# Lag attention on sums and differences of mirrored rows

## The chip, the cores and the metric

The kernel runs on one core of one Trainium2 chip. The metric is the device time of one execution in microseconds; the time before is 1598.67 us, the median of three runs (1595.01 to 1599.94).

## The reference

Two blocks of a gated cross-attention model run on x (8 batches, 256 positions, 1024 features) and a context of the same shape. The change lies in the first operation only, an attention over lags: the normalised x is correlated with the context along the sequence in each feature, the eleven largest lags of the 256 are found, softmaxed, and used to add up shifted copies of the context.

```python
qf = jnp.fft.fft(q, axis=2)
kf = jnp.fft.fft(k, axis=2)
corr = jnp.fft.ifft(qf * jnp.conj(kf), axis=2).real
topk = int(C * np.log(L))                     # 11, with C = 2 and L = 256
w, idx = jax.lax.top_k(corr.transpose(0, 1, 3, 2), topk)
w = jax.nn.softmax(w, axis=-1)
for i in range(topk):
    g = jnp.minimum(idx[:, :, None, :, i] + pos, L - 1)
    out = out + w[:, :, None, :, i] * jnp.take_along_axis(v, g, axis=2)
...
x = x + jnp.tanh(g_xattn[0]) * _L0_xattn_ref(_layernorm(x, axis=-1), ctx_4096, ctx_4096)
x = x + jnp.tanh(g_ffn[0]) * _L0_ffn_ref(...)      # 16 experts, 2 per token
x = x + jnp.tanh(g_xattn[1]) * _L1_xattn_ref(...)  # attention over the context
x = x + jnp.tanh(g_ffn[1]) * _L1_ffn_ref(...)      # quantised feed-forward
```

After that come a mixture of experts, a softmax attention over the context, and a quantised feed-forward. Rows (positions) are independent of each other in all of these but for the pairing of a batch's queries with its own context.

## The kernel before

x stays in SBUF for the whole kernel (tile X, 16 tiles of 128 rows by 1024). The function lag_attention treats 16 units: a unit u is a batch b = u // 2 and a half h of the features (512 columns, C). The Fourier transforms are float32 matrix products with tables held in `tab`. Each product of a 128x128 table with 512 columns appears in the profile as two records, and all of them are issued by the helper at L52.

One unit passes through these steps. `spectra` on the tensor engine (L454) transforms the context (v_raw) and the normalised queries (q_n): the table has four kinds (even cosine, even sine, odd cosine, odd sine) and the 256 rows are two blocks, so 8 products for the context (4 for the even kinds, then 4 for the odd ones, into the same PSUM banks 2 and 3) and 4 for the queries (banks 0 and 1). The scalar engine copies the context's spectra into `vs` (L276 to L289; the even ones are four instructions and signal v_ev1). `c_products` on the vector engine (L340) multiplies the spectra, `c_sums` on GpSimd (L233) adds them, `correlate` (L473) transforms back to lags, `lags_out` (L291) copies the result to `corr`. `top_lags` on the vector engine (L347) works on four groups c of 128 features: two rounds of the eight largest, masking, and `finish`, which multiplies the exponentials (`exponent`, scalar engine, L297) by a mask, takes the reciprocal of the sum and scales (L360). `turn_weights` (L484) transposes the weights by the tensor engine, `weights_out` (L302) copies them, `weight_spectra` (L492) transforms them by 8 products into banks 4 to 7. `o_products` (L398) multiplies these with `vs` in 8 instructions, `o_sum` (L241) adds pairs on GpSimd, `positions` (L500) transforms back to rows by 8 products, and `add` (L408) adds the result to X. Each second unit the vector engine also forms the layer-norm tables of a batch (`variance`, `tables`), for the first norm of a batch to come or for the running norm of a batch that is done; one power on GpSimd lies between the two.

Each engine's order is written out by hand in its function `step`; in a step `now` is unit u, `before` is u-1, `after` is u+1, `next2` is u+2:

```python
# vector engine: top_lags(now) in two halves, o_products(before) between them,
#                c_products(after), add(before), variance and tables
# tensor engine: spectra(after), positions(before), turn_weights(now),
#                correlate(after), weight_spectra(now)
# scalar engine: lags_out(now) x2, exponent(now) 0 and 1, spectra(after, even),
#                exponent(now) 2 and 3, spectra(after, odd), normalise(next2) x2, weights_out(now)
# GpSimd:        o_sum(before) x4, c_sums(after), powers of the norms
```

An instruction waits for semaphores only; an engine never passes a waiting instruction. In particular `spectra(after, even)` on the scalar engine waits until all 8 `o_products(before)` are done, since both units use the same slot of `vs` (the units u-1 and u+1 have the same h), and `c_products(after)` waits for v_ev1. At the start the whole `tab` (3584 columns, 1.8 MB) comes in one transfer, ahead of the gate's value.

## Time and profile before

| | |
|---|---|
| median of three runs | 1598.67 us |
| the profiled execution | 1598.1 us, span 1596.4 us |
| lag attention in it | from the start to about 529 us |
| tensor engine busy in the span | 1360.1 us (85%) |
| vector engine busy | 797.0 us (50%) |
| scalar engine busy | 523.3 us (33%) |
| GpSimd busy | 428.1 us (27%) |

The busy shares are means over stages that differ. In lag attention the pattern of a unit repeats about every 30 us. A row of the timeline merges equal neighbouring instructions: the first number is the start, the second the time from the first one's start to the last one's end, "x8" how many, and in brackets is how long the engine stood idle before and what released it. "PEclk" is the tensor engine's granted clock as a share of 2.4 GHz: 1.00 is 2.4 GHz, 0.50 is 1.2 GHz. A row of windows gives the stretch and its length, then busy time (and instructions) of the tensor engine's matmuls, its weight loads, the vector engine, the scalar engine and GpSimd, then the granted clock, the DMA share and GB/s.

### The profile page before, as it was taken

To read this page: it belongs to the slowest core of one execution; us is meant where nothing else is said; L and a number is where in the kernel's file an instruction comes from. 1 tells how busy PE (TensorE), PEld (TensorE's weight loads), DVE (VectorE), ACT (ScalarE), POOL (GpSimd) and SP (SyncE) were. 2 spreads that over 40 slices of the span, in tenths; PEclk is the share of its full clock that TensorE was granted. 3 is DMA by queue.
4 is the path that set the end of the run, shared out by engine and by line. 5 is a ranking of instruction groups with operands and counts; after the bars stand their busy time and mean duration, and the time that the engine had idled before them with its cause. 6 is when DMAs were issued, how large, how long until landed. Compare 5 with 4: busy or idle time off the path is not lost. (4 is left out here: it accounts for less than half of the span.)

```text
span 1596.4 us, 19695 instructions
## 1 busy us (share of the span) xinstructions
PE 1360.1 (85%) x6035; PEld 894.1 (56%) x6041; DVE 797.0 (50%) x2181; ACT 523.3 (33%) x827; POOL 428.1 (27%) x481
## 2 busy tenths in 40 slices
PE   5999999999996799898888788259999999927886
PEld 2454454454452674346666576158888888714443
DVE  3678778778774444002122122265444442227996
ACT  2322322322320420004344344322222222148884
POOL 1223223223222002502111112361111100035885
PEclk9999999999997868999899999679999999968999
DMA  4210210400200623005667665433332321060111
GB/s 178 79 54 27 79 53 26 171 13 14 93 1 0 226 94 104 15 0 184 191 209 234 207 216 184 156 92 118 106 101 87 101 67 53 27 217 27 53 53 79
DMA packets 53378, 159.14 MB, mean 100 GB/s; under 512 B 7120, under 2 KB 15312, under 8 KB 53200
## 3 DMA queue, kind: packets, MB, share of 16 engines
q1 hardware_dynamic: 41792, 120.20, 21.4%
q0 software_dynamic: 11536, 38.30, 8.1%
q8 instruction: 28, 0.46, 0.1%
q14 instruction: 22, 0.18, 0.0%
HBM read 112.82 MB, written 45.66 MB: 99 GB/s over the span
## 5 line engine op out<-in xcount | busy, mean ns | idle before, releaser
L44 PE MATMUL xa_bank<-xa_xT_hi,M_hi 128*128 128x256 f32 x512 | 153.7, 300 | 0.0
L46 PE MATMUL xa_bank<-xa_xT_hi,M_lo 128*128 128x256 f32 x512 | 144.2, 282 | 0.0
L45 PE MATMUL xa_bank<-xa_xT_lo,M_hi 128*128 128x256 f32 x512 | 144.2, 282 | 0.0
L52 PE MATMUL la_bank<-la_v_raw,la_tab 128*128 128x512 f32 x256 | 118.5, 606 | 29.5 <-ACT la_v_spec L285 16.3
L1026 PEld LDWEIGHTS ex_bank<-ex_gu,ex_xT 128*128 128x128 f32 x624 | 119.6, 194 | 22.4 <-issue 20.9
L52 PE MATMUL la_bank<-la_osum,la_tab 128*128 128x512 f32 x256 | 117.4, 613 | 13.8 <-POOL la_osum L246 13.8
L1026 PE MATMUL ex_bank<-ex_gu,ex_xT 128*128 128x224 f32 x624 | 127.3, 358 | 0.7 <-ACT ex_xT L961 0.7
L246 POOL TENSOR_TENSOR la_osum<-la_oprod 128x512 f32<-128x512 f32 x64 | 82.7, 1313 | 153.4 <-DVE la_oprod L405 153.4
L52 PE MATMUL la_bank<-la_wT,la_tab 128*128 128x512 f32 x256 | 112.6, 592 | 1.2 <-ACT la_wT L306 1.2
L52 PEld LDWEIGHTS la_bank<-la_v_raw,la_tab 128*128 128x128 f32 x256 | 48.0, 192 | 96.1 <-issue 55.8
L1212 ACT ACTIVATE xa_A<-xa_bank,shift 128x256 f32<-128x256 f32 x64 | 30.3, 473 | 209.7 <-PE xa_bank L46 209.7
L44 PEld LDWEIGHTS xa_bank<-xa_xT_hi,M_hi 128*128 128x128 f32 x512 | 97.0, 189 | 2.8 <-issue 1.7
L45 PEld LDWEIGHTS xa_bank<-xa_xT_lo,M_hi 128*128 128x128 f32 x512 | 97.0, 190 | 2.5 <-issue 1.7
L46 PEld LDWEIGHTS xa_bank<-xa_xT_hi,M_lo 128*128 128x128 f32 x512 | 96.8, 189 | 0.0
L988 DVE COPY ex_xT<-ex_bank 128x512 f32<-128x512 f32 x40 | 27.7, 692 | 138.4 <-PE ex_bank L1008 138.4
L1038 PE MATMUL ex_bank<-ex_dn,ex_silu_then_turned 112*128 112x512 f32 x156 | 83.1, 658 | 14.3 <-ACT ex_silu_then_turned L973 14.3
L52 PEld LDWEIGHTS la_bank<-la_osum,la_tab 128*128 128x128 f32 x256 | 50.2, 197 | 78.8 <-issue 63.3
L602 PE MATMUL ex_bank<-Wk,Wq 128*128 128x512 f32 x192 | 88.7, 624 | 6.5 <-issue 4.8
L405 DVE TENSOR_TENSOR la_oprod<-la_bank,la_v_spec 128x512 f32<-128x512 f32 x128 | 80.1, 685 | 18.2 <-PE la_bank L52 7.8
L933 POOL TENSOR_TENSOR ex_current<-ex_listed,ex_nought 128x1 int32<-128x1 int32 x41 | 7.7, 188 | 271.6 <-PE ex_bank L1008 268.6
L52 PEld LDWEIGHTS la_bank<-la_wT,la_tab 128*128 128x128 f32 x256 | 48.6, 190 | 55.8 <-issue 53.6
L999 DVE COPY ex_y<-ex_bank 128x512 f32<-128x512 f32 x39 | 27.0, 692 | 102.7 <-ACT ex_y L976 102.7
(264 smaller groups left out, 2684.5 us busy)
## 6 DMA issues: line engine op xcount, KB each, us to landing
produced<-ex_y SPq DMA_DIRECT2D x39, 512.0 KB, 3.0
ex_gu<-in_gate_up SPq DMA_DIRECT2D x16, 896.0 KB, 6.2
X<-in_x SPq DMA_DIRECT2D x8, 1024.0 KB, 7.1
la_v_raw<-in_ctx SPq DMA_DIRECT2D x16, 512.0 KB, 4.3
produced<-la_zeros SPq DMA_DIRECT2D x16, 512.0 KB, 5.2
normal<-rt_xn SPq DMA_DIRECT2D x16, 512.0 KB, 3.6
xa_fT<-in_ctx_T SPq DMA_DIRECT2D x8, 1024.0 KB, 5.6
xa_f<-in_ctx SPq DMA_DIRECT2D x8, 1024.0 KB, 5.0
```

The costliest lines, as they stand in the source:

```text
L44: pe.matmul(out, a[0], b[0], start=first, stop=False)
L45: pe.matmul(out, a[0], b[1], start=False, stop=False)
L46: return pe.matmul(out, a[1], b[0], start=False, stop=last)
L52: return pe.matmul(out, a, b, start=first, stop=last)
L246: pool.tensor_tensor(osum[:, i, :], oprod[:, a, :], oprod[:, a + 1, :], ALU.add if i % 2 == 0 else ALU.subtract).then_inc(s["osums"], 1)
L405: dve.tensor_tensor(oprod[:, 2 * (i % 2) + k, :], bank[bk][:], vs[:, h, vk, :], ALU.mult).then_inc(s["oprods"], 1)
L602: last = pe.matmul(out, W[1][:, k, (n // 2) * P:(n // 2 + 1) * P], W[0][:, k, (n % 2) * 512:(n % 2 + 1) * 512], start=(k == 0), stop=(k == ...
L988: dve.tensor_copy(xT[:, 4:8, :].rearrange("p a b -> p (a b)"), bank[3][:]).then_inc(s["xT_dve"], 1)
L999: dve.tensor_copy(y[:, 512:1024], bank[5][:]).then_inc(s["y_dve"], 1)
L1026: m = pe.matmul(bank[0][:, 0:UP_COLS], xT[:, k, :], gu[:, slot, k * UP_COLS:(k + 1) * UP_COLS], start=(k == 0), stop=(k == KD - 1))
L1038: m = pe.matmul(bank[4 + i][:], hT, dn[:, slot, i * 512:(i + 1) * 512], start=True, stop=True)
L1212: act.activation(A[:, m % AHEAD, :], bank[2 + m % 2][:, 0:L], ACT.Identity, bias=shift[:, m:m + 1]).then_inc(s["a_out"], 1)
```

## The change

The second half of every batch (rows 128 to 255) of x and of the context is laid down in falling order before the launch, and the result is turned back after it. Row p of the one block then lies beside its mirror image in the other, so the cosine kinds need only the sum of the blocks and the sine kinds only the difference. GpSimd forms the sums and differences of context, queries and weights (`v_halves`, `q_halves`, `w_halves`). What the mirror does not cover (the last row of the context, lag 0 and lag 128) goes in by products with a single row, and one by a full product with `sign_t`. The back transform gives two banks, whose sum is one block and whose difference is the other: `add` has four instructions, not two. Products (each is two records) per unit: context 8 to 6 (two of them with one row), queries 4 to 2, weights 8 to 6 (one with one row), positions 8 to 4.

The scaling of the weights (L360) goes from the vector to the scalar engine (`share`), `c_products` moves into the middle of `top_lags`, `correlate` ahead of `turn_weights`, `lags_out` to the step before, `positions` starts when two of the four sums are there, and the table comes in two transfers (896 columns, then 1664).

```diff
+        v_less = sb("v_less", [P, 2, C])
+        q_less = sb("q_less", [P, C])
+        w_less = sb("w_less", [P, 4, P])
...
-            sp.dma_start(tab[:], tables).then_inc(s["tab_in"], 16)
+            sp.dma_start(tab[:, 0:LAGS_AT], tables[:, 0:LAGS_AT]).then_inc(s["tab_in"], 16)
             sp.dma_start(graw[:], column(gate, 0)).then_inc(s["gate_in"], 16)
             load_v(1, 0, 1)
+            sp.dma_start(tab[:, LAGS_AT:], tables[:, LAGS_AT:]).then_inc(s["tab_rest"], 16)
...
+            def v_halves(u, b, h):
+                pool.wait_ge(v_in[h], 16 * (b + 1))
+                pool.tensor_tensor(v_less[:, h, :], v_raw[:, h, 0, :], v_raw[:, h, 1, :], ALU.subtract).then_inc(s["v_fold"], 1)
+                pool.tensor_tensor(v_raw[:, h, 0, :], v_raw[:, h, 0, :], v_raw[:, h, 1, :], ALU.add).then_inc(s["v_fold"], 1)
+            def q_halves(u):
+                pool.wait_ge(s["q_ready"], 2 * u + 2)
+                pool.tensor_tensor(q_less[:], q_n[:, 0, :], q_n[:, 1, :], ALU.subtract).then_inc(s["q_fold"], 1)
+                pool.tensor_tensor(q_n[:, 0, :], q_n[:, 0, :], q_n[:, 1, :], ALU.add).then_inc(s["q_fold"], 1)
+            def w_halves(u, g):
+                pool.wait_ge(s["wdone"], 4 * u + 2 * g + 2)
+                two = slice(2 * g, 2 * g + 2)
+                a, b = wt[:, two, 1:P], wt[:, two, P + 1:L]
+                pool.tensor_tensor(w_less[:, two, 1:P], a, b, ALU.subtract).then_inc(s["w_fold"], 1)
+                pool.tensor_copy(w_less[:, two, 0:1], wt[:, two, P:P + 1]).then_inc(s["w_fold"], 1)
+                pool.tensor_tensor(a, a, b, ALU.add).then_inc(s["w_fold"], 1)
...
             def step(on, due):                      # GpSimd
+                if next2:
+                    v_halves(*next2)
                 if before:
                     for i in range(4):
                         o_sum(before[0], i)
                 if after:
                     c_sums(after[0])
+                if now:
+                    w_halves(now[0], 0)
+                    w_halves(now[0], 1)
+                if next2:
+                    q_halves(next2[0])
...
-                at_least(act, s["wdone2"], 4 * u)
+                at_least(act, s["wdone2"], 4 * (u - 1) + 2 * g + 2)
...
+            def share(u, c):
+                act.wait_ge(s["wrec"], 4 * u + c + 1)
+                act.activation(wt[:, c, :], wt[:, c, :], ACT.Identity, scale=wrec[:, c:c + 1]).then_inc(s["wdone"], 1)
...
             def step(on, due):                      # scalar engine
                 if now:
-                    lags_out(now[0], 0)
-                    lags_out(now[0], 1)
                     exponent(now[0], 0)
                     exponent(now[0], 1)
                 if after:
                     spectra(after[0], after[2], False)
                 if now:
-                    exponent(now[0], 2)
-                    exponent(now[0], 3)
+                    share(now[0], 0)
                 if after:
                     spectra(after[0], after[2], True)
                 if next2:
                     for j in range(2):
                         normalise(*next2, j)
                 if now:
+                    exponent(now[0], 2)
+                    share(now[0], 1)
+                    exponent(now[0], 3)
+                    share(now[0], 2)
+                if after:
+                    lags_out(after[0], 0)
+                if now:
+                    share(now[0], 3)
+                if after:
+                    lags_out(after[0], 1)
+                if now:
                     weights_out(now[0])
...
-                    return dve.tensor_scalar(w, w, wrec[:, c:c + 1], None, ALU.mult)
...
-                    count("wdone", finish(c - 1, 2))
+                    dve.memset(spare[:], 0.0)
...
+                for i, signs in enumerate(((tg, tg), (tg, less_tg))):
+                    if i:
+                        at_least(dve, s["half_added"], 2 * u + 2)
+                    for j in range(2):
+                        xs = X[:, bass.ds(2 * b + j, 1), halfsl(h)]
+                        made = dve.scalar_tensor_tensor(out=xs, in0=bank[4 + i][:].rearrange("p (a c) -> p a c", a=1), scalar=signs[j][:, 0:1],
+                                                        in1=xs, op0=ALU.mult, op1=ALU.add)
...
                 def output_spectra():
                     if before:
                         o_products(before[0], before[2])
+                    if after:
+                        c_products(after[0], after[2])
                 if now:
                     lags(now[0], output_spectra)
                 else:
                     output_spectra()
-                if after:
-                    c_products(after[0], after[2])
...
+                at_least(pe, s["v_fold"], 2 * u + 2)
                 at_least(pe, s["corr_sb"], 2 * u)
+                full_product(pe, bank[2][:], rows_t(0), more, True, False)
+                full_product(pe, bank[2][:], last_t(0), last, False, True)
+                full_product(pe, bank[3][:], rows_t(1), less).then_inc(s["spec_v1"], 1)
+                at_least(pe, s["q_fold"], 2 * u + 2)
                 at_least(pe, s["prods"], 4 * u)
+                full_product(pe, bank[0][:], rows_t(0), q_n[:, 0, :])
+                full_product(pe, bank[1][:], rows_t(1), q_less[:]).then_inc(s["spec_q"], 1)
                 at_least(pe, s["v_ev1"], u + 1)
+                full_product(pe, bank[2][:], rows_t(2), more, True, False)
+                full_product(pe, bank[2][:], last_t(1), last, False, True)
+                full_product(pe, bank[3][:], rows_t(3), less).then_inc(s["spec_v2"], 1)
...
-                at_least(pe, s["wdone"], 5 * u + 5)
+                at_least(pe, s["w_fold"], 6 * u + 6)
...
+                full_product(pe, bank[4][:], lags_t(0), more, True, False)
+                full_product(pe, bank[4][:], last_t(2), first, False, True)
+                full_product(pe, bank[5][:], lags_t(1), less, True, False)
+                full_product(pe, bank[5][:], sign_t, more, False, True)
+                full_product(pe, bank[6][:], lags_t(2), more)
+                full_product(pe, bank[7][:], lags_t(3), less).then_inc(s["wspec"], 1)
...
+                for i, (j, first) in enumerate(((0, True), (1, True), (1, False), (0, False))):
+                    at_least(pe, s["osums"], 4 * u + max(i, 1) + 1)
+                    m = full_product(pe, bank[4 + j][:], pos_t(i), osum[:, i, :], first, not first)
...
                 if before:
                     positions(before[0])
+                if after:
+                    correlate(after[0])
                 if now:
                     turn_weights(now[0])
-                if after:
-                    correlate(after[0])
-                if now:
                     weight_spectra(now[0])
```

## Rows read from the trace of the kernel before

**Rows 1.** The page: its first line.
```profile
span 1596.4 us, 19695 instructions
```
**Rows 2.** Busy time by windows: the steady part, then one stretch after an idle time.
```profile
200.00:300.00 100.00, 95.95 (x278) 49.61 (x277) 79.85 (x274) 29.35 (x54) 25.83 (x22) 1.00 0.25 92
486.80:490.80 4.00, 3.98 (x5) 1.71 (x6) 3.76 (x17) 0.51 (x1) 0.00 (x0) 0.55 0.00 0
```
**Rows 3.** Timeline of one unit, vector engine.
```profile
241.84 2.48 DVE L405 TENSOR_TENSOR la_oprod<-la_bank,la_v_spec 128x512 f32<-128x512 f32 x4
246.95 0.49 DVE L356 SCALAR_TENSOR_TENSOR la_wt<-la_rest,la_wt 128x256 f32<-128x256 f32 x1
249.14 0.36 DVE L360 TENSOR_SCALAR la_wt<-la_wt,la_wrec 128x256 f32<-128x256 f32 x1
249.41 0.09 DVE L380 MATCH_VALUE_LOAD la_rest<-la_nextv,la_rest 128x8 f32 x1
249.92 0.43 DVE L356 SCALAR_TENSOR_TENSOR la_wt<-la_rest,la_wt 128x256 f32<-128x256 f32 x1
253.76 2.48 DVE L345 TENSOR_TENSOR la_prod<-la_bank,la_v_spec 128x512 f32<-128x512 f32 x4
259.97 1.41 DVE L412 SCALAR_TENSOR_TENSOR X<-la_bank,la_tg,X 128x512 f32 x2 [3.73 <-PE la_bank L52]
261.30 0.69 DVE L564 BATCH_NORM_STATS2 first_ln_stats<-X 128x6 f32 x1
266.66 0.06 DVE L352 MEMSET la_spare<- 128x1 f32 x1 [0.37 <-issue]
271.89 2.48 DVE L405 TENSOR_TENSOR la_oprod<-la_bank,la_v_spec 128x512 f32<-128x512 f32 x4
```
**Rows 4.** The same unit, tensor engine.
```profile
241.00 3.60 PE L52 MATMUL la_bank<-la_v_raw,la_tab 128*128 128x512 f32 x8
249.23 3.70 PE L52 MATMUL la_bank<-la_v_raw,la_tab 128*128 128x512 f32 x8 [1.20 <-ACT la_v_spec L285]
252.77 7.03 PE L52 MATMUL la_bank<-la_osum,la_tab 128*128 128x512 f32 x16
259.64 1.04 PE L489 MATMUL la_bank<-la_ident,la_wt 128*128 128x128 f32 x8
```
**Rows 5.** The same unit, scalar engine.
```profile
247.07 0.60 ACT L281 ACTIVATE la_v_spec<-la_bank 128x512 f32<-128x512 f32 x1 [6.63 <-DVE la_oprod L405]
252.97 0.60 ACT L288 ACTIVATE la_v_spec<-la_bank 128x512 f32<-128x512 f32 x1 [1.54 <-PE la_bank L52]
253.94 1.51 ACT L274 ACTIVATE la_q_n<-X,first_ln_shift,first_ln_scale 128x512 f32 x2
```
**Rows 6.** The same unit, GpSimd.
```profile
243.21 2.50 POOL L246 TENSOR_TENSOR la_osum<-la_oprod 128x512 f32<-128x512 f32 x2 [7.70 <-DVE la_oprod L405]
245.88 2.69 POOL L246 TENSOR_TENSOR la_osum<-la_oprod 128x512 f32<-128x512 f32 x2 [0.17 <-DVE la_oprod L405]
```
**Rows 7.** Timeline, tensor engine, work that follows an idle time.
```profile
21.98 5.40 PE L52 MATMUL la_bank<-la_q_n,la_tab 128*128 128x512 f32 x8 [4.15 <-ACT la_q_n L274]
50.64 5.11 PE L52 MATMUL la_bank<-la_tab,la_cross 128*128 128x256 f32 x16 [2.67 <-POOL la_cross L239]
486.82 8.89 PE L52 MATMUL la_bank<-la_osum,la_tab 128*128 128x512 f32 x16 [7.08 <-POOL la_osum L246]
511.64 10.13 PE L52 MATMUL la_bank<-la_osum,la_tab 128*128 128x512 f32 x16 [6.74 <-POOL la_osum L246]
```
**Rows 8.** Timeline: the start, and the output products of units 0, 13 and 15.
```profile
14.74 0.20 ACT L265 ACTIVATE la_tg<-la_graw 128x1 f32<-128x1 f32 x1 [12.63 <-DMA la_graw<-in_g_xattn]
62.71 2.48 DVE L405 TENSOR_TENSOR la_oprod<-la_bank,la_v_spec 128x512 f32<-128x512 f32 x4 [2.91 <-issue]
450.47 2.48 DVE L405 TENSOR_TENSOR la_oprod<-la_bank,la_v_spec 128x512 f32<-128x512 f32 x4 [2.91 <-issue]
504.93 2.48 DVE L405 TENSOR_TENSOR la_oprod<-la_bank,la_v_spec 128x512 f32<-128x512 f32 x4 [7.77 <-PE la_bank L52]
```

More of the change, by code:

```diff
@@ L66, in fourier_tables, with kinds, mirrored @@
 def fourier_tables():
-    t = np.arange(L)[:, None].astype(np.float64)
+    w = np.pi / L
+    p = np.arange(P)[:, None].astype(np.float64)
     k = np.arange(P)[None, :].astype(np.float64)
-    even, odd = 2 * np.pi * t * k / L, np.pi * t * (2 * k + 1) / L
-    alternate = (-1.0) ** np.arange(L)
-    seq = np.stack([np.cos(even), np.sin(even), np.cos(odd), np.sin(odd)], 1)
-    inverse = seq.copy() * 2.0
-    seq[:, 1, 0] = alternate
-    inverse[:, 0, 0] = 1.0
-    inverse[:, 1, 0] = alternate
-    ext = seq.copy()
-    ext[L - 1, 0, 0] += L
-    ext[L - 1, 2:] -= seq[:, 2:].sum(0)
-    lag = inverse[:, :2] / L
-    pos = inverse / (2 * L)
-    pos[:, 1, 0] *= -1.0
-    seq, ext = (x.reshape(2, P, 4, P).transpose(1, 0, 2, 3).reshape(P, -1) for x in (seq, ext))
-    lag, pos = (x.transpose(2, 1, 0).reshape(P, -1) for x in (lag, pos))
-    return np.concatenate([seq, ext, lag, pos], 1).astype(np.float32)
-TABLE_COLS = 2 * 4 * P * 2 + 2 * L + 4 * L
+    sign = (-1.0) ** np.arange(P)
+    def kinds(at):
+        return np.stack([np.cos(2 * k * w * at), np.sin(2 * k * w * at), np.cos((2 * k + 1) * w * at), np.sin((2 * k + 1) * w * at)], 1)
+    middle = p - (L - 1) / 2
+    rows = kinds(middle)
+    rows[:, 1, 0] = np.sin(np.pi * middle[:, 0])
+    last = np.zeros((3, P, P))
+    last[0, 0, 0] = L
+    last[1, 0] = -2 * rows[:, 2].sum(0)
+    last[2, 0] = sign
+    lags = kinds(p)
+    lags[:, 1, 0] = 0
+    lags[0, 1, 0] = 1
+    lags[0, 3] = -sign
+    found = np.concatenate([P + np.arange(P), (P - np.arange(P)) % P])[None, :]
+    angle = 2 * np.pi * p * found / L
+    lag = np.stack([2 * np.cos(angle), 2 * np.sin(angle)], 0) / L
+    lag[0, 0] = 1 / L
+    lag[1, 0] = (-1.0) ** found[0] / L
+    pos = kinds(p + 0.5).transpose(1, 2, 0) * 2
+    pos[0, 0] = 1
+    pos[1, 0] = -np.sin(np.pi * (p[:, 0] + 0.5))
+    pos /= 2 * L
+    parts = [rows.reshape(P, -1), *last, lags.reshape(P, -1), lag.transpose(1, 0, 2).reshape(P, -1),
+             pos.transpose(1, 0, 2).reshape(P, -1), sign[:, None] * (k == 0)]
+    return np.concatenate(parts, 1).astype(np.float32)
+ROWS_AT, LAST_AT, LAGS_AT, LAG_AT, POS_AT, SIGN_AT = 0, 4 * P, 7 * P, 11 * P, 11 * P + 2 * L, 15 * P + 2 * L
+TABLE_COLS = SIGN_AT + P
+def mirrored(x):
+    return np.concatenate([x[:, :P], x[:, P:][:, ::-1]], 1)
 def lag_attention(nc, x, ctx, gate, tables, Wk, Wk_home, X, scales_after, produced):
@@ L249, in step @@
             def step(on, due):
-                before, after = on(-1), on(1)
+                before, now, after, next2 = on(-1), on(0), on(1), on(2)
+                if next2:
+                    v_halves(*next2)
                 if before:
@@ L308, in step @@
             def step(on, due):
-                before, now, after, next2 = on(-1), on(0), on(1), on(2)
+                now, after, next2 = on(0), on(1), on(2)
                 if now:
-                    lags_out(now[0], 0)
-                    lags_out(now[0], 1)
                     exponent(now[0], 0)
@@ L409, in add @@
                 at_least(dve, s["out_pe"], u + 1)
-                for j in range(2):
-                    xs = X[:, bass.ds(2 * b + j, 1), halfsl(h)]
-                    i = dve.scalar_tensor_tensor(out=xs, in0=bank[4 + j][:].rearrange("p (a c) -> p a c", a=1), scalar=tg[:, 0:1], in1=xs, op0=ALU.mult, op1=ALU.add)
-                i.then_inc(s["added"], 1)
+                for i, signs in enumerate(((tg, tg), (tg, less_tg))):
[5 more added lines that the diff above has]
+                                                        in1=xs, op0=ALU.mult, op1=ALU.add)
+                        if i == 0:
+                            made.then_inc(s["half_added"], 1)
+                made.then_inc(s["added"], 1)
             def lags(u, between):
```

75 lines of the change are left out of this document (30 added, 45 removed).

## The prediction, on record before the changed kernel ran

> **What bounds the kernel now.** I read the page for the span [rows 1], then the busy times of a steady stretch, then the timelines of one unit engine by engine, since the change touches lag attention alone. In the steady stretch the tensor engine is busy 95.95 of 100 us at granted clock 1.00, the vector engine 79.85, the scalar engine 29.35, GpSimd 25.83 [rows 2]. A unit lasts (450.47 - 62.71) / 13 = 29.83 us [rows 8]. The tensor engine sets it, but the vector engine is close: its only long wait in a unit is 3.73 us before the add [rows 3]. So whatever is taken from the tensor engine, a unit can't fall below 29.83 - 3.73 = 26.1 us unless the vector engine's own path shortens. From here the argument is about that path.
>
> **The change, part by part.**
>
> Tensor engine. A record costs 0.43 us (252.77 to 259.64 is 16 of them [rows 4]). Context 16 to 12, queries 8 to 4, weights 16 to 12, positions 16 to 8: 20 records fewer, 8.6 us a unit. I price a product with one row like a full one, as its 512 columns pass all the same; at nothing, three of them would give 2.6 us more. Its work falls to about 28.6 - 8.6 = 20.0 us (28.6 is 96% of a unit [rows 2]), so it no longer sets the unit by its sum, only by what waits for it.
>
> Vector engine, work. Gone: L360, which costs 0.27 us at each of three places (249.14 to 249.41 [rows 3]) and 0.36 at the fourth: -1.2 us. New: two more adds, 1.33 us (259.97 to 261.30 [rows 3]), and the wait that orders them after the first pair, bounded by nothing and 0.3; I take 0.1: +1.4. Extra memsets of 0.06 us [rows 3] vanish behind their neighbours. 26.1 - 1.2 + 1.4 = 26.3 us.
>
> Vector engine, first new wait. c_products(after) moves from the end of top_lags to right behind o_products(before). It needs v_ev1, and the four copies that give v_ev1 wait on the scalar engine for the last of those same o_products: L281 begins at 247.07, after an idle time of 6.63 us released by L405 [rows 5], and the tensor engine, which waits for the same signal, starts at 249.23 [rows 4]. Before, 6.8 us of top_lags (246.95 to 253.76 [rows 3]) hid these copies; now nothing does. The vector engine stands from 246.95 to 249.23: +2.3 us. Queued behind it are c_products, the second half of top_lags and all that the weights need. If the copies could start earlier it would be nothing; I see no reason.
>
> Second new wait. exponent(2) now stands on the scalar engine behind spectra(odd) and two normalises, and finish(2) in group c = 3 needs it. Count from the start of o_products (0 = 241.84). c_products start at 7.4 and end at 9.8 (four take 2.48 [rows 3]). Group c = 2 takes 249.92 - 246.95 - 0.27 = 2.7 us, so finish(2) is due at 12.5. On the other side the odd products start at 7.4, six records and the hop take 2.9 (eight took 252.97 - 249.23 = 3.74 [rows 4, 5]), the two copies 1.0 (252.97 to 253.94), the normalises 1.4 of their 1.51 [rows 5], the exponential half of a 0.60 us copy plus a fixed part, about 0.5: 13.2. The vector engine waits 0.7 us. Sum at full clock: 26.3 + 2.3 + 0.7 = 29.3 us.
>
> Clock. The tensor engine finishes the first context products and the queries early and then stands until v_ev1. The weights' chain of the unit before ends about 2.9 us before o_products start (worked out below), then come 10 records, 4.3 us: it is done at 1.4 and idles until 7.4, 6 us in every unit; now this idle time is 1.20 [rows 4]. After idle times of 7.08, 6.74 and 4.15 us the work took 8.89 and 10.13 us where 16 records take 7.03, and 5.40 where 8 take 3.60: 1.9, 3.1 and 1.8 us more [rows 4, 7], and 486.8 to 490.8 shows 0.55, nearly all at 1.2 GHz [rows 2]. The bounds are nothing (the steady stretch stays at 1.00) and, for the six odd records that the second wait hangs on, their own length, 2.6 us. I take 1.9, the row nearest in kind: 16 records after 7.08 us. The unit becomes 31.2 us against 29.83: **+1.4 us**.
>
> The weights' chain, which takes the place of the tensor engine's sum: finish(3) ends near 16.5 at full clock, share 0.5, w_halves 1.5, transposes 1.04 [rows 4], two copies 1.1, twelve records 5.2, hops 0.6: 26.4 of 29.3 us. So it has 2.9 us to spare. w_halves is new: a 512-column sum takes 1.25 [rows 6], so two sums of 254 and a copy are 1.5 if cost follows columns, 3.8 if none does; the spare time covers that. The shares on the scalar engine (4 x 0.5 on 29%) and v_halves and q_halves on GpSimd (4 x 1.25 us, making some 16 us of 31) run while the vector engine does adds, norm tables and the first groups. The powers of the norms are queued behind q_halves, which end near 21 us, before the variance does near 22: nothing. correlate, moved ahead, is done near 17 and its result is used at 24: nothing.
>
> Here the Trainium skill (SBUF — State Buffer, "Who interferes with whom") speaks against the change: a vector instruction with two SBUF inputs and a GpSimd instruction that reads SBUF exclude each other for a whole instruction. The row: the masked product at 246.95, beside o_sum, took 0.49 against 0.43 us, and that pair of sums 2.69 against 2.50 [rows 3, 6]. By the row GpSimd's doubled work costs 0.1 us a unit, which I leave out; by the rule two of the four masked products could wait 1.25 us each.
>
> The start. Before, the gate's value came behind 1.8 MB of tables and released the vector engine at 14.74 [rows 8]. Now 0.46 MB goes ahead of it, 1.3 MB less; with q_halves (2.5 us) in the path and fewer records against it, I take 4 us less until o_products(0); bounds 0 and 7.
>
> The end. Units 13 to 15: the step of 13 has no norm tables, so the chain sets it (26.4 + 1.9 + a hop = 28.4, -1.4); the next two intervals took 54.46 [rows 8] and become 31.2 + 23.0 = 54.2, the 23.0 from 5.1 + 5.8 for products and groups, 10 for the chain and 2 for the clock: -0.3. After o_products(15) positions ended at 521.8, 16.9 us later [rows 7, 8]. Now the last sum comes at 6.7 and 8 records at 1.2 GHz, half begun earlier, end near 11; the adds cost 1.4: -4.5.
>
> Sum against the profiled execution, 1598.1 us (1.7 of it outside the span): -4 + 12 x 1.4 - 1.4 - 0.3 - 4.5 = +6.6, so **1605 us**. The median shown is 1598.67, 0.6 above that execution. The rest of the kernel sees rows in another order and otherwise the same work: nothing. Half the products, and nothing gained, because the two new waits and the clock take it back.
>
> **Rivals.**
>
> B: the clock costs the unit little (the six records run mostly at 2.4 GHz, or what they lose hides behind the first wait). For it: 100 us at 1.00 with short idle times [rows 2]. Against: every idle time above 4 us in lag attention was followed by slow records [rows 7]. Then a unit is 29.3, 13 of them give -6, the chain in the unit without norm tables -3, start -4, the end some -10: **1575**. It decides from a delay of the odd records below 1.1 us (1598.1 - 10 + 13 x (29.3 + d - 29.83) = 1598).
>
> C: the two waits of the vector engine don't occur, by an order of signals that I misread. Then 26.3 a unit: 14 x -3.5 - 12 = **1537**. Against it: the releaser in rows 5.
>
> D, slower: the weights' chain sets the period. It decides when it grows by its 2.9 us to spare. Place: between correlate and weight_spectra the tensor engine has two short idle times (about 1.7 and 1.2 us) with transposes between. After 2.67 us idle, 16 records of 256 columns, the columns of eight that took 3.60, took 5.11 [rows 4, 7]. If the twelve records lose 3.1 and w_halves take 1.5 us more, the period is 26.4 + 1.9 + 4.6 = 32.9: 13 x 3.1 - 10 = +30, **1628**.
>
> E: the port rule as told. 2.5 us a unit on top of the forecast: 1605 + 14 x 2.5 = **1640**. That each GpSimd row shows a few tenths at most speaks against it.
>
> **Chances.** Forecast 0.50 (own range 1595 to 1614), B 0.22, C 0.07, D 0.17, E 0.04. The range takes the forecast, B whole and D's lower half: 1573 to 1623. From no change 0.3% can be told, 1594 to 1603.5. Of the forecast's half, 0.17 falls in there and 0.05 below: faster 0.05 + 0.22 + 0.07 = 0.34, same 0.17, slower 0.28 + 0.17 + 0.04 = 0.49.
>
> **What would show it.** Right: the vector engine idles about 2.3 us before c_products, released by L285's copy, and some 2.6 us before finish(2), released by the exponential; the tensor engine idles 6 us a unit before the odd context products, and lag attention shows a mean granted clock well under 1; its busy time per unit at 2.4 GHz is near 20 us; the unit is 31 us; the adds follow with no wait. Wrong: a unit under 29.3 us, no idle time before c_products, clock 1.00 after these idle times, or o_products waiting for the weight spectra, which would be D.

## The result

The changed kernel takes **1662.54 us** (median of 4 runs, 1659.87 to 1673.58) against 1596.84 (1592.98 to 1599.94) for the kernel before on the same chip: ratio 1.0426, 95% interval 1.0372 to 1.048. It is slower, as the odds said, but by 66 us instead of 7, and lies above the range. The page of the changed kernel, its first lines; the granted clock of the first third is what differs most:

```profile
span 1662.0 us, 19330 instructions
PE 1336.2 (80%) x5721; PEld 849.6 (51%) x5721; DVE 837.2 (50%) x2198; ACT 551.3 (33%) x891; POOL 555.1 (33%) x641
PEclk9788787878878776989999999959999999968999
```

The same windows as in [rows 2], then one behind an idle time (columns: busy time of PE, PEld, DVE, ACT, POOL, granted clock, DMA share, GB/s):

```profile
200.00:300.00 100.00, 78.89 (x170) 34.26 (x169) 75.33 (x234) 30.39 (x58) 45.12 (x49) 0.81 0.13 42
284.90:288.90 4.00, 4.00 (x5) 1.00 (x5) 3.82 (x10) 0.33 (x1) 2.51 (x2) 0.50 0.00 0
```

No engine is the bound by its sum any more: in 100 us every engine idles over 20, and the tensor engine works at 0.81 of its clock. One unit on the vector engine, the answer to [rows 3]:

```profile
242.67 2.48 DVE L466 TENSOR_TENSOR la_oprod<-la_bank,la_v_spec 128x512 f32<-128x512 f32 x4
245.34 2.52 DVE L466 TENSOR_TENSOR la_oprod<-la_bank,la_v_spec 128x512 f32<-128x512 f32 x4 [0.19 <-POOL la_osum L291]
250.20 2.49 DVE L411 TENSOR_TENSOR la_prod<-la_bank,la_v_spec 128x512 f32<-128x512 f32 x4 [2.34 <-ACT la_v_spec L337]
259.18 0.43 DVE L422 SCALAR_TENSOR_TENSOR la_wt<-la_rest,la_wt 128x256 f32<-128x256 f32 x1 [3.80 <-ACT la_wt L352]
262.47 2.19 DVE L476 SCALAR_TENSOR_TENSOR X<-la_bank,la_tg,X 128x512 f32 x3
269.30 1.21 DVE L644 TENSOR_TENSOR running_ln_small<-running_ln_small 128x2 f32<-128x2 f32 x1 [0.83 <-POOL running_ln_small L622]
270.54 1.19 DVE L646 TENSOR_TENSOR running_ln_small<-running_ln_small 128x2 f32<-128x2 f32 x1
277.50 2.48 DVE L466 TENSOR_TENSOR la_oprod<-la_bank,la_v_spec 128x512 f32<-128x512 f32 x4
```

The unit is 277.50 - 242.67 = 34.83 us. Two waits stand where the prediction put them, 2.34 and 3.80 us (2.3 and 2.6 told), and the adds follow without one. What was not priced are two products of 128x2 elements in the norm tables that take 1.2 us each. GpSimd at that time:

```profile
268.55 0.71 POOL L622 TENSOR_TENSOR running_ln_small<-running_ln_small 128x2 f32<-128x2 f32 x1 [0.75 <-DVE running_ln_small L639]
269.23 1.26 POOL L260 TENSOR_TENSOR la_v_less<-la_v_raw 128x512 f32<-128x512 f32 x1
270.45 1.26 POOL L261 TENSOR_TENSOR la_v_raw<-la_v_raw 128x512 f32<-128x512 f32 x1
```

Each tiny product ends when a v_halves operation ends (269.30 + 1.21 = 270.51, 270.54 + 1.19 = 271.73). In the kernel before, with GpSimd at rest, the same two products (here in the tables of a first norm) took:

```profile
265.11 0.16 DVE L577 TENSOR_TENSOR first_ln_small<-first_ln_small 128x2 f32<-128x2 f32 x1 [0.81 <-POOL first_ln_small L555]
265.31 0.16 DVE L579 TENSOR_TENSOR first_ln_small<-first_ln_small 128x2 f32<-128x2 f32 x1
```

The tensor engine of the changed kernel, the answer to [rows 4], with the idle time of the next unit as well:

```profile
250.05 4.07 PE L52 MATMUL la_bank<-la_v_raw,la_tab 128*128 128x512 f32 x4 [4.89 <-ACT la_v_spec L337]
254.06 2.08 PE L52 MATMUL la_bank<-la_v_less,la_tab 128*128 128x512 f32 x2
255.93 5.06 PE L52 MATMUL la_bank<-la_osum,la_tab 128*128 128x512 f32 x8
267.74 5.81 PE L52 MATMUL la_bank<-la_wT,la_tab 128*128 128x512 f32 x12 [1.18 <-ACT la_wT L363]
284.88 4.07 PE L52 MATMUL la_bank<-la_v_raw,la_tab 128*128 128x512 f32 x4 [6.65 <-ACT la_v_spec L337]
```

After 4.89 us idle (6 told) the six odd context records take 256.14 - 250.05 = 6.1 us instead of 2.6. The scalar engine's row on which the exponential hangs, and the exponential:

```profile
256.17 0.60 ACT L340 ACTIVATE la_v_spec<-la_bank 128x512 f32<-128x512 f32 x1 [5.77 <-PE la_bank L52]
258.55 0.50 ACT L352 ACTIVATE la_wt<-la_corr,la_neg_max 128x256 f32<-128x256 f32 x1
```

**Where the 66 us are.** The output products of units 0, 13 and 15, to be set against [rows 8]:

```profile
67.13 2.48 DVE L466 TENSOR_TENSOR la_oprod<-la_bank,la_v_spec 128x512 f32<-128x512 f32 x4 [2.09 <-issue]
520.37 2.49 DVE L466 TENSOR_TENSOR la_oprod<-la_bank,la_v_spec 128x512 f32<-128x512 f32 x4 [5.88 <-PE la_bank L52]
577.11 2.48 DVE L466 TENSOR_TENSOR la_oprod<-la_bank,la_v_spec 128x512 f32<-128x512 f32 x4 [12.31 <-PE la_bank L52]
590.57 0.69 DVE L631 BATCH_NORM_STATS2 running_ln_stats<-X 128x6 f32<-128x512 f32 x1
```

| | before | after | difference | predicted |
|---|---|---|---|---|
| until o_products(0) | 62.71 | 67.13 | +4.4 | -4 |
| 13 units | 387.76 | 453.24 | +65.5 | +15.4 |
| two intervals to o_products(15) | 54.46 | 56.74 | +2.3 | -0.3 |
| from there to the norm | 18.33 | 13.46 | -4.9 | -4.5 |
| the rest | 1073.1 | 1071.4 | -1.7 | 0 |

### The profile page after: what moved, and what is told of

Same layout as the page of the kernel before. It is cut to its first block and busy times, and to the rows that moved or that the text cites. A ratio compares the mean times of both kernels' runs of the same rounds, so it can differ in the third digit from the quotient of the medians.

```text
span 1662.0 us, 19330 instructions
## 1 busy us (share of the span) xinstructions
PE 1336.2 (80%) x5721; PEld 849.6 (51%) x5721; DVE 837.2 (50%) x2198; ACT 551.3 (33%) x891; POOL 555.1 (33%) x641
## 5 line engine op out<-in xcount | busy, mean ns | idle before, releaser
L52 PE MATMUL la_bank<-la_v_raw,la_tab 1*128 1x512 f32 (+1 forms) x128 | 97.9, 873 | 95.8 <-ACT la_v_spec L337 77.8
L52 PEld LDWEIGHTS la_bank<-la_v_raw,la_tab 1*128 1x128 f32 (+1 forms) x128 | 26.7, 248 | 152.1 <-ACT la_v_spec L337 90.8
L52 PE MATMUL la_bank<-la_osum,la_tab 128*128 128x512 f32 x128 | 80.3, 785 | 8.7 <-POOL la_osum L291 8.7
L52 PEld LDWEIGHTS la_bank<-la_wT,la_tab 128*128 128x128 f32 x192 | 39.6, 229 | 85.5 <-issue 62.9
L352 ACT ACTIVATE la_wt<-la_corr,la_neg_max 128x256 f32<-128x256 f32 x64 | 32.4, 506 | 127.1 <-DVE la_neg_max L434 127.1
```

Source lines behind the costliest of these rows:

```text
L52: return pe.matmul(out, a, b, start=first, stop=last)
L352: act.activation(wt[:, c, :], corr[:, c, :], ACT.Exp, bias=neg_max[:, c:c + 1]).then_inc(s["exed"], 1)
```

## The experiments

All ratios are to the kernel before, on the same chip. The loads of the start land at different times from profile to profile, so starts are compared by what the engines wait for.

**1. v_halves behind c_sums on GpSimd.** The sum and difference of the next context rows leave the stretch of the norm tables.

```
-                if next2:
-                    v_halves(*next2)
                 if before: ... o_sum
                 if after:
                     c_sums(after[0])
+                if next2:
+                    v_halves(*next2)
```

> Only GpSimd's order differs from the changed kernel: the sums and differences of the context stand behind the cross sums, no longer first in the step. Theory (GpSimd's operation holds up a vector instruction that reads two operands in SBUF, here the tiny products of the norm tables, 1.21 and 1.19 us where they took 0.16): these products fall back to 0.16 us, a unit from 35.0 to 32.9 us, the whole kernel from 1662.5 to about 1635 us. Rival (the tables are slow for another reason, such as the power on GpSimd coming late): the two products stay at 1.2 us and the time stays within 3 us of 1662.5.

Measured: 1628.96 us, ratio 1.0246 (1.0198 to 1.0293), so 1.7% less than the change as it was, as told. The vector engine in this kernel:

```profile
258.97 0.16 DVE L644 TENSOR_TENSOR running_ln_small<-running_ln_small 128x2 f32<-128x2 f32 x1 [0.83 <-POOL running_ln_small L622]
259.16 0.16 DVE L646 TENSOR_TENSOR running_ln_small<-running_ln_small 128x2 f32<-128x2 f32 x1
```

Same instructions, same inputs, 0.16 us again: what GpSimd runs beside them was the whole cause of their 1.2 us. A unit takes 32.79 us on average over 13, against 34.86. This agrees with the Trainium skill (SBUF — State Buffer, "Who interferes with whom"): the vector engine's second SBUF port is GpSimd's, held exclusively. The same rule was weighed in the prediction, at another instruction.

**2. The one-row products on 128 rows.** The tables hold zeros in the other 127 rows of these columns, so the sums are the same.

```
-            return tab[0:1, LAST_AT + kind * P:LAST_AT + (kind + 1) * P]
+            return table(LAST_AT + kind * P, P)
...
-                more, less, last = v_raw[:, h, 0, :], v_less[:, h, :], v_raw[0:1, h, 1, :]
+                more, less, last = v_raw[:, h, 0, :], v_less[:, h, :], v_raw[:, h, 1, :]
...
-                more, less, first = wT[:, 0, :], wT[:, 1, :], wT[0:1, 1, :]
+                more, less, first = wT[:, 0, :], wT[:, 1, :], wT[:, 1, :]
```

> The three products with a single row (1x128 by 1x512) read all 128 rows; the table is zero in the other 127, so the sums are the same. Theory (the switch between one row and 128 rows costs: a load does not slip under the product before it, 4.0 us for four records at 1.2 GHz where 3.4 would do): the six odd records take 0.7 us less, a unit 34.3, the kernel about 1652 us. Rival (a product with one row costs like a full one, as the prediction had it): within 2 us of 1662.5.

Measured: 1644.05 us, ratio 1.0358 (1.0307 to 1.041); as told. The wait before finish(2) fell from 3.80 to 2.90:

```profile
249.13 0.42 DVE L422 SCALAR_TENSOR_TENSOR la_wt<-la_rest,la_wt 128x256 f32<-128x256 f32 x1 [2.90 <-ACT la_wt L352]
```

Six odd records with one-row products among them are dearer than six full ones, not equal. From the first one's start to the start of the work behind them they took 255.93 - 250.05 = 5.88 us in the changed kernel and 245.92 - 240.90 = 5.02 here; of the difference at most 0.2 is the clock, which came back at the end of the six here. The weight loads of the changed kernel show where the rest lies:

```profile
252.06 0.50 PEld L52 LDWEIGHTS la_bank<-la_v_raw,la_tab 1*128 1x128 f32 x2 [1.50 <-issue]
254.06 0.50 PEld L52 LDWEIGHTS la_bank<-la_v_less,la_tab 128*128 128x128 f32 x2 [1.50 <-issue]
```

The loads come in pairs, and at each change from 128 rows to one and back the next pair begins 2.0 us after the last, behind 1.50 us without a load; in this experiment each load follows the one before by 0.86 us, behind 0.52 us. So the price is seen at the change of shape, on both sides of it; whether products with one row would be dear among themselves was not tried.

**3. Filler for the idle time.** The query products are made four times over (12 records more), then five times (16 more), so that the tensor engine doesn't stand.

```
-                full_product(pe, bank[0][:], rows_t(0), q_n[:, 0, :])
-                full_product(pe, bank[1][:], rows_t(1), q_less[:]).then_inc(s["spec_q"], 1)
+                for _ in range(4):
+                    full_product(pe, bank[0][:], rows_t(0), q_n[:, 0, :])
+                    m = full_product(pe, bank[1][:], rows_t(1), q_less[:])
+                m.then_inc(s["spec_q"], 1)
```

> The two query products are issued four times instead of once (12 records more, the same results written again), so the tensor engine works through most of the 6.65 us in which it stood before the odd context products. Theory (that idle time puts the tensor engine to 1.2 GHz and the six odd records, on which finish(2) hangs, run at half speed): the odd records take about 3.3 us instead of 6.1 until the copy that follows, the wait before finish(2) falls from 3.8 to about 1 us, a unit to 32.2, the kernel to about 1623 us in spite of 5 us more tensor work a unit. Rival (the tensor engine's time is not what finish(2) waits for, or the clock doesn't depend on that idle time): no change, or slower by the added work where it is not hidden.

Measured: 1653.86 us, ratio 1.0431: missed. In most units 2.1 us of idle time were left, and the clock fell all the same (0.50 from 254 to 258 us); in four of the thirteen 0.6 us or less was left, the clock stayed at 1.00, and these units took 32.0 to 32.3 us, as told. A unit of the first kind:

```profile
251.82 3.83 PE L52 MATMUL la_bank<-la_v_raw,la_tab 128*128 128x512 f32 x4 [2.12 <-ACT la_v_spec L337]
```

> The two query products are issued five times instead of once (16 records more, 6.9 us, same results). With 12 records more an idle time of 2.1 to 2.2 us was left before the odd context products and the granted clock still fell to 0.50 in most units; where none was left it stayed at 1.00 and the wait before finish(2) was gone. Theory (that idle time, down to some 2 us, costs the clock, and the clock costs the unit): now it is gone in nearly every unit, the six odd records take about 3.3 us up to the copy behind them, the wait before finish(2) is 1 us or less, a unit about 32.3 us and the ratio to the kernel before 1.015 to 1.025, where the changed kernel has 1.043. Rival (the clock falls whatever the filler does): ratio 1.04 or more.

Measured: 1657.74 us, ratio 1.044 (1.0395 to 1.0484): missed as a time, but it shows the term. In the units where the clock stayed at 1.00, the wait before finish(2) is 0.95 us (prediction at full clock: 0.7) and the unit 282.75 - 250.50 = 32.25; but at its end the clock fell behind the transposes instead, twelve weight records took 10.67 us, and in the next unit, of 36.04 us, c_products waited for the filler:

```profile
264.17 0.42 DVE L422 SCALAR_TENSOR_TENSOR la_wt<-la_rest,la_wt 128x256 f32<-128x256 f32 x1 [0.95 <-ACT la_wt L352]
271.99 10.67 PE L52 MATMUL la_bank<-la_wT,la_tab 128*128 128x512 f32 x12 [1.17 <-ACT la_wT L363]
294.33 2.48 DVE L411 TENSOR_TENSOR la_prod<-la_bank,la_v_spec 128x512 f32<-128x512 f32 x4 [6.39 <-PE la_bank L52]
```

So the clock is worth some 2.8 us at the wait before finish(2), and filler isn't a way to have them. Filler also stands in the start, where o_products(0) came at 78.10 us instead of 67.13; that took back what the units gave (33.9 us on average instead of 34.86).

**4. The exponentials first on the scalar engine.** exponent(2) ahead of the odd copies, exponent(3) ahead of the normalises.

```
                 if now:
                     share(now[0], 0)
+                    exponent(now[0], 2)
                 if after:
                     spectra(after[0], after[2], True)
+                if now:
+                    share(now[0], 1)
+                    exponent(now[0], 3)
                 if next2: ... normalise
                 if now:
-                    exponent(now[0], 2)
-                    share(now[0], 1)
-                    exponent(now[0], 3)
                     share(now[0], 2)
```

> Only the scalar engine's order differs from the changed kernel: exponential 2 before the copies of the odd spectra, exponential 3 before the two normalises. Theory (finish(2) waits 3.8 us only because exponential 2 stands behind the odd copies and the normalises): that wait goes, some 0.2 us is left before finish(3), a unit takes 31.3 us and the kernel about 1613 us; the chain of the weights then has under 1 us to spare. Rival (the odd copies are needed as soon, so the wait moves to the output products, released by the tensor engine): the unit stays above 34 us.

Measured: 1645.64 us, ratio 1.0374 (1.0317 to 1.0431): mostly missed. The wait before finish(2) is gone, and a unit takes only 1.1 us less. What was behind the wait came up: the positions, late by the same slow clock, and again the port, where an instruction of the norm that took 0.17 us now meets q_halves:

```profile
254.11 2.20 DVE L477 SCALAR_TENSOR_TENSOR X<-la_bank,la_tg,X 128x512 f32 x3 [1.83 <-PE la_bank L52]
259.94 0.81 DVE L640 TENSOR_SCALAR running_ln_small<-running_ln_mv 128x2 f32<-128x2 f32 x1
```

**5. c_products between groups 2 and 3.**

```
                 for c in range(4):
                     if c == 2:
                         between()
+                    if c == 3:
+                        later()        # c_products(after)
...
```

> c_products are issued one group later than in the changed kernel, after group 2 of top_lags, whose 2.7 us then cover the four copies. Theory of the prediction (the wait before c_products costs 2.3 us of its own): the wait goes and a unit falls to 32.7, ratio about 1.022. Theory now (both waits hang on one path: copies, odd products, odd copies, normalises, exponential 2, which takes 11 us from the end of the output products, whatever the vector engine does meanwhile): the wait before c_products goes and the wait before finish(2) grows by as much, to about 6.1 us; ratio 1.04 to 1.045, unchanged.

Measured: 1682.46 us, ratio 1.0591 (1.054 to 1.0641). The unit did as told (35.06 us): the wait before c_products vanished and the one before finish(2) grew from 3.80 to 5.95. They are one path through the scalar engine's copies, not two terms. But the whole was 1.6% slower, by a row that neither theory had:

```profile
248.99 0.06 DVE L418 MEMSET la_spare<- 128x1 f32 x1 [6.47 <-issue]
270.45 0.43 DVE L422 SCALAR_TENSOR_TENSOR la_wt<-la_rest,la_wt 128x256 f32<-128x256 f32 x1 [5.95 <-ACT la_wt L352]
```

Every second unit, at the turn of the batch loop, the vector engine stands 6.5 us with nothing to wait for that the profile shows (a loop's trip is two units). The row of instruction packets on the page went from 22 (first line, the changed kernel) to 42:

```profile
q14 instruction: 22, 0.18, 0.0%
```
```profile
q14 instruction: 42, 0.34, 0.1%
```

**6. All four edits (1, 2, 4, 5), with filler, and with positions early instead.** The second moves positions(before) ahead of the odd context products on the tensor engine, where its sums are ready first and the work fills the idle time.

```
                 full_product(pe, bank[1][:], rows_t(1), q_less[:]).then_inc(s["spec_q"], 1)
+                between()          # positions(before[0])
                 at_least(pe, s["v_ev1"], u + 1)
```

> Four changes together: GpSimd forms the context's sums after the cross sums, the one-row products read all rows, exponentials 2 and 3 stand before the normalises, c_products after group 2; and 12 filler records (query products issued four times). Theory: no wait is left on the vector engine's path; a unit is its work, 5.1 + 2.7 + 2.4 + 3.3 + 3.0 + 5.1 + 5.0 = 26.6 us against 29.8 of the kernel before; clock 1.00; ratio about 0.97. Rival (the chain of the weights or the tensor engine's order sets the unit by then): unit above 29 us, ratio 0.99 or more, and the output products or the adds wait for the tensor engine.

> As the kernel with all four changes, but without filler records: the tensor engine does positions(before) ahead of the odd context products, so real work stands in the idle time, which shrinks to the 2.5 us until two output sums are there. Theory: in units where the clock still falls after these 2.5 us positions and the odd products run at 1.2 GHz and the adds or exponential 3 wait 1 to 3 us; unit 27 to 29.5 us, ratio 0.975 to 1.0, behind the kernel with filler. Rival (2.5 us don't matter): as fast as the kernel with filler or faster.

Measured: 1603.36 us, 1.0085 (1.0052 to 1.0117) with filler, missed; 1583.84 us, 0.9967 (0.9937 to 0.9997) with positions early, within what was told. The second is the first version that is not slower than the kernel before, by its interval 0.0 to 0.6% faster; both still carry 6.2 us at `issue` at the loop's turns.

**7. The loop's turn.** By my count in the compiled program the loop of the vector engine has 234 instructions in all kernels, and moving c_products had put one instruction more ahead of it; no trace shows this count. One kernel adds only that to the change, the other takes one away from the best version.

```
             dve.wait_ge(x_in, 16)
+            dve.memset(spare[:], 0.0)
             norm.variance(dve, X, 0)
```

> The changed kernel with one memset of 128x1 more on the vector engine, before its batch loop (0.06 us of work, once). Open is what the 6.2 to 6.5 us are in which the vector engine stood at 'issue' at each turn of the loop in the three kernels that put c_products between groups 2 and 3. Theory 'place in the instruction stream': their loop (234 instructions in all kernels) began one instruction later, so that its branch back needs instructions that are no longer at hand; then this kernel has the same stall with nothing else changed: 5 turns by some 6.2 us, +30 us, ratio to the kernel before 1.060, and a row of 6 us at 'issue' once in two units. Rival 'the order of work' (the stall comes from the moved products themselves): ratio unchanged, 1.04 to 1.045, and no such row.

Measured: 1679.83 us, ratio 1.0544 (1.0484 to 1.0604). The row is there, from one memset of 0.06 us, four times (the loop's five trips have four turns back; I had counted five). Waits at the memset that opens a unit's groups (columns: total, times, longest):

```profile
DVE la_spare L418 <- issue: 25.2, 4, 6.4
```

Its span is 17.9 us over the changed kernel's: from o_products(0) to the last of them it takes 23.9 us more, the start is 2.2 shorter, and the rest (-3.8) lies in later stages and was not looked into. The queue of instruction packets moves 23 packets between 90 and 450 us, against 4 in the changed kernel, and 4 of them in the 9 us around the turn before 246.88 us: instructions are being brought in while the engine stands. Taking the instruction away again:

```
-            dve.wait_ge(s["tgd"], 1)
-            link(dve.tensor_scalar(less_tg[:], tg[:], -1.0, None, ALU.mult))
...
+            pool.wait_ge(s["tgd"], 1)
+            pool.tensor_scalar(less_tg[:], tg[:], -1.0, None, ALU.mult).then_inc(s["signed"], 1)
```

> The kernel with the four edits and positions before the odd context products (0.9967 of the kernel before), with one thing more: the negated gate column is made on GpSimd instead of the vector engine, so that the vector engine has one instruction less before its batch loop. Theory 'place in the instruction stream': the 6.2 us at 'issue' at five turns go, -31 us, ratio 0.975 to 0.98. Rival 'the order of work': ratio stays at 0.995 to 1.0.

Measured: **1553.78 us, ratio 0.9778 (0.9726 to 0.9829)**. Waits at the same memset:

```profile
DVE la_spare L419 <- issue: 1.9, 5, 0.4
```

The place of the loop in the stream was the cause of the stall, as the one memset shows by itself; the order of work was not. Of the 31 us between the two spans (1578.3 and 1547.4), 23 are the turns and 7 the start: the vector engine no longer stands until the gate has landed, and its first statistics begin when X is there, at 5.83 us instead of 11.96:

```profile
11.76 0.15 DVE L405 TENSOR_SCALAR la_less_tg<-la_tg 128x1 f32<-128x1 f32 x1 [10.80 <-ACT la_tg L317]
```
```profile
5.83 0.06 DVE L639 MEMSET first_ln_small<- 128x2 f32 x1 [4.88 <-DMA X<-in_x]
```

The Trainium skill (Runtime: NRT & Kernel Launch, "Instruction fetch mechanics") says that instructions are fetched in blocks of 256, two of them held, and that a taken branch out of these two has to wait for a fetch. The runs agree in kind: the same loop either returns within 0.4 us or waits 6.2 to 6.5 us, by its place alone, and packets are fetched at those turns. Which place is the edge no run here shows, only that one instruction crossed it.

**8. c_products back at the change's place, the rest as in 6.**

> The changed kernel with v_halves behind c_sums, the one-row products on 128 rows, the exponentials 2 and 3 early and positions before the odd context products; c_products stay where the change had them, behind o_products and ahead of group 2, and the loop stands where it stood. Theory 'one path' (the wait before c_products and that before finish(2) are one wait on ScalarE's copies, and moving c_products only moves it): within 1% of the kernel with c_products between groups 2 and 3 once that has no stall, 0.975 to 0.99. Rival 'two waits': c_products wait some 2 us each unit beside the path, +26 us, 0.99 to 1.0.

Measured: 1593.61 us, ratio 1.0023 (0.9993 to 1.0053): above both theories. Thirteen units take 30.51 us each, against 28.12 with c_products between the groups. Here 2.34 us stand before c_products and nothing before finish(2):

```profile
287.64 2.48 DVE L412 TENSOR_TENSOR la_prod<-la_bank,la_v_spec 128x512 f32<-128x512 f32 x4 [2.34 <-ACT la_v_spec L337]
```
```profile
262.16 2.48 DVE L412 TENSOR_TENSOR la_prod<-la_bank,la_v_spec 128x512 f32<-128x512 f32 x4 [0.29 <-DVE la_rest L446]
```

(First this kernel, then the best one.) "One path" held only as long as exponential 2 stood behind the odd copies; with that gone, the wait before c_products is a term of its own: 13 x 2.4 = 31 us. Another 10 us are the start (o_products(0) at 65.76 and 56.02), most of it the gate's value, for which this kernel still waits.

**9. The first context rows ahead of the first norm on GpSimd.**

```
+            v_halves(0, 0, 0)
             norm.on_pool(pool, 0)
```

> The kernel of e10_loop_back with GpSimd's sum and difference of the first unit's context rows ahead of its part of the first norm, as soon as the rows have landed. Theory 'the start is late by GpSimd's order': the first context product on the tensor engine starts some 3 us earlier than at 17.2 us, and the port no longer holds the first norm's tables (2.1 us); the query products follow the tables, so the whole comes out 2 to 3 us shorter, ratio 0.001 to 0.002 below e10_loop_back, at the edge of what can be told by the time and plain in the profile. Rival (the context rows land after the norm): no change.

Measured: 1558.74 us, ratio 0.9794 (0.9725 to 0.9864): no gain. The context products start 3.3 us earlier than in the best version (10.34 instead of 13.65), then wait for the queries, and o_products(0) come at 57.49 instead of 56.02. The 1.5 us are the clock: the twelve weight records before them begin 0.2 us earlier (50.29 and 50.51) and take 7.11 us at a granted clock of 0.76, against 5.42 at 1.00. What was first was not what the start waits for:

```profile
16.72 2.07 PE L52 MATMUL la_bank<-la_q_n,la_tab 128*128 128x512 f32 x2 [2.17 <-POOL la_q_n L265]
```

## Why the prediction was wrong

- **The mechanism was right**: half the products, and the time given back by two waits and the clock; the tensor engine no longer sets the unit. The wait before c_products was 2.34 us (2.3 told), group by group the busy time agrees, the adds wait for nothing, the end came out at -4.9 (-4.5 told).
- **The term "nothing" for GpSimd's work beside the norms was the largest step that failed.** The prediction asked when GpSimd's queue reaches the norm's power ("before the variance does": nothing), and not what it does behind it: v_halves of the next but one unit start 0.7 us later, beside the tables. +2.1 us a unit, 27 us in all; experiment 1 gives them back. Rival E had the rule and its price was fair (2.5 us a unit), but it was tied to the masked products, and set at 0.04 on the ground that rows of the kernel before showed a few tenths. Those masked products started as a GpSimd operation was ending. The row showed a lucky phase, not a cheap port.
- **The clock term was mis-sized**: 1.9 us taken, while the odd records took 6.1 us where six at full clock take 2.6. The row chosen [rows 7] was one in which 16 records outlast the slow stretch; six lie in it whole and lose 2.6, the prediction's far bound (the other 0.9 of the 3.5 is mostly the next point). That it is the clock and not the order on the scalar engine, experiment 3 shows: at 1.00 the same wait is 0.95 us.
- **"A product with one row like a full one" failed**: with the changes to one row and back the six odd records take some 0.7 us more at 1.2 GHz. Experiment 2 took 0.9 us off the wait, with what the clock gave, and 0.7% off the kernel.
- **The sum treated the two waits as separate terms.** That did no harm to the sum while both stood, but it hid that moving c_products alone is worth nothing (experiment 5), that taking away only the exponential's delay uncovers the positions (experiment 4), and that afterwards the first wait is a term after all (experiment 8).
- **The start failed in sign**: +4.4 instead of -4. That less data goes ahead of the gate was right (its reader starts at 9.66 instead of 15.06 us). Overlooked was that v_halves stand behind the first norm on GpSimd, and that the first tables then meet the same port; the tensor engine began only at

```profile
17.21 4.05 PE L52 MATMUL la_bank<-la_v_raw,la_tab 128*128 128x512 f32 x4 [17.21 <-POOL la_v_raw L261]
```

 Experiment 9 shows that this alone was not the price either, since the queries come later still. A further part is the clock: sixteen correlate records of the second unit took 6.54 us at a granted clock of 0.56, where the kernel before took 5.11 [rows 7]. How the rest of the 8 us splits was not settled. Experiment 7 took away a cost that both kernels have, the vector engine's wait for the gate's value (8.71 us here, 14.11 before).
- **D** (the weights' chain) did not happen: the vector engine waited for weight spectra only before o_products 13 and 15. **B** asked for the clock to be kept: in the units of experiment 3 where it was, the unit is 32.25 us, 2.1 of them the port, so 30.1 against B's 29.3.

From 29.3 us (the prediction at full clock) to 34.83: 3.1 at the wait before finish(2), most of it the clock and some of it the one-row products; 2.1 the port; 0.2 the adds; 0.1 elsewhere.

**What the version that wins does.** It keeps the halved products and moves each cost found above: v_halves out of the tables' way, full-row products, exponentials ahead of copies, c_products where their inputs are ready, positions into the idle time, the gate off the vector engine's start, and the loop back on its place. 28.12 us a unit against 29.83, 1553.78 us against 1590.10 (2.2%). In this version only the place of c_products was tried by itself (experiment 8), and the loop and the gate together (experiment 7); how the other edits share the gain is not shown. The kernel before waits for the gate's value as well and was not given that edit, so the part of the 2.2% that the start gives, some 7 us, is not the halved products' merit. Its clock still falls in the gap around the transposes:

```profile
272.04 0.65 PE L562 MATMUL la_bank<-la_ident,la_wt 128*128 128x128 f32 x4 [1.97 <-POOL la_wt L278]
272.53 0.60 PE L562 MATMUL la_bank<-la_ident,la_w_less 128*128 128x128 f32 x4
274.30 8.36 PE L52 MATMUL la_bank<-la_wT,la_tab 128*128 128x512 f32 x12 [1.18 <-ACT la_wT L365]
```

Twelve records take 8.36 us there instead of 5.2; the vector engine then waits 0.58 us before o_products. What lies behind that wait was not tried.

## What to carry to other kernels

When work moves to GpSimd, list for each operation what the vector engine runs beside it, down to 128x2 products: what counts is how long GpSimd's instruction still runs, not the length of the one that waits. When work leaves the tensor engine, price what follows the new idle time at 1.2 GHz for its whole length if it is short, and fill the gap by reordering real work. And before a slower variant is blamed on its order, look at the rows released by `issue` at a loop's turn.

## What the hardware showed unexpectedly

- 2.12 us of idle time were enough for the granted clock to fall to 0.50 (experiment 3); the prediction had seen it from 2.67 up. In the best version, 1.97 and 1.18 us idle with 1.1 us of transposes between did it too.
- A vector instruction of 0.16 us took 1.21 beside a 1.26 us GpSimd instruction; one of 0.17 us with a single tile as input took 0.81 (experiment 4).
- At 2.4 GHz, six records with one-row products among them took 276.35 - 273.39 = 2.96 us (the changed kernel, first fence), six full ones 255.47 - 252.90 = 2.57 (the best version).

```profile
273.39 2.07 PE L52 MATMUL la_bank<-la_v_raw,la_tab 128*128 128x512 f32 x4
276.35 1.02 PE L52 MATMUL la_bank<-la_q_n,la_tab 128*128 128x512 f32 x2
```
```profile
252.90 1.88 PE L52 MATMUL la_bank<-la_v_raw,la_tab 128*128 128x512 f32 x4
255.47 1.02 PE L52 MATMUL la_bank<-la_q_n,la_tab 128*128 128x512 f32 x2
```

- One instruction more ahead of a loop cost some 6 us at each of its four turns, 24 us in all, with 19 more instruction packets over the same stretch.
